# Cross-attention maxima in another order, with down tiles and late queries between them, in a fused two-layer decoder kernel

## The reference, cut to what matters

```python
x = x + block_attention(layernorm(x))            # 16 heads of 16, causal inside blocks of 64 tokens, rotary q and k
x = x + cross_attention(layernorm(x), ctx, ctx)  # below
x = x + ffn(layernorm(x))                        # routed experts, and a shared gated FFN
...
q = (Q @ Wq + bq).reshape(B, L, H, E)            # H = 16 heads, E = 16
k = (K @ Wk + bk).reshape(B, S, H, E)
scores = jnp.einsum('blhe,bshe->bhls', q, k)
A = jax.nn.softmax(scale * scores, axis=-1)
out = jnp.einsum('bhls,bshd->blhd', A, v).reshape(B, L, H * E) @ We + be
...
shared = jax.nn.gelu(sg, approximate=False) * su @ Sd.T
```

## Time and profile before

| | |
|---|---|
| median of 3 runs | 3006.3 us (3000.59 to 3008.07) |
| the profiled execution's own time | 3005.41 us |
| its span in the profile | 3003.6 us |
| mean granted clock of TensorE | 0.928 of full |
| busy: PE, PEld, DVE, ACT, POOL | 89%, 53%, 48%, 36%, 23% |
| span of the second layer's four batches | about 1740 to 2540 us |

### The profile page before, as it was taken

How to read it: one execution, slowest core, us unless ns; L and a number is a source line. 1 busy time by engine, 2 the same in 40 slices (tenths; PEclk the granted TensorE clock), 3 DMA queues, 4 the chain that set the end, 5 groups by cost and what they waited for, 6 DMA issues and landing times. The chain is left out here.

```text
span 3003.6 us, 40190 instructions
## 1 busy us (share of the span) xinstructions
PE 2674.7 (89%) x16417; PEld 1586.3 (53%) x16417; DVE 1450.4 (48%) x2233; ACT 1085.8 (36%) x1885; POOL 682.3 (23%) x364
## 2 busy tenths in 40 slices
PE   7679999999999999999959969989989898699997
PEld 4255534754275425653248844453552543487776
DVE  5565346832875366733711135445444553644432
ACT  4673245622563255523412223343434433011111
POOL 0255034900663055702520020000000000022222
PEclk8889999999999999999969977998989998799999
DMA  5540002100030003100059810010100102044442
GB/s 193 215 163 22 0 1 109 44 1 0 7 138 8 1 1 118 35 0 1 8 209 348 324 45 8 8 29 8 22 22 1 22 8 87 17 150 149 168 163 67
DMA packets 62127, 219.26 MB, mean 73 GB/s; under 512 B 12293, under 2 KB 28122, under 8 KB 45178
## 3 DMA queue, kind: packets, MB, share of 16 engines
q1 hardware_dynamic: 45802, 187.39, 17.3%
q0 software_dynamic: 9568, 18.75, 2.5%
q10 hardware_dynamic: 6576, 10.57, 1.0%
HBM read 172.50 MB, written 39.99 MB: 71 GB/s over the span
## 5 line engine op out<-in xcount | busy, mean ns | idle before, releaser
L642 PE MATMUL psum<-arena 128*128 128x256 f32 (+7 forms) x4224 | 1109.0, 414 | 65.4 <-ACT arena L1500 11.5
L642 PEld LDWEIGHTS psum<-arena 128*128 128x128 f32 (+1 forms) x4224 | 690.4, 199 | 433.9 <-issue 320.3
L2460 POOL TENSOR_TENSOR arena<-arena 128x1024 f32<-128x1024 f32 x128 | 300.1, 2386 | 111.7 <-DVE arena L1963 96.4
L1963 DVE TENSOR_TENSOR_SCAN arena<-arena,psum 128x512 f32<-128x512 f32 x256 | 291.5, 1201 | 26.3 <-PE psum L783 18.1
L783 PEld LDWEIGHTS psum<-arena 128*128 128x128 f32 x2048 | 243.0, 198 | 47.6 <-ACT arena L1530 40.3
L783 PE MATMUL psum<-arena 128*128 128x128 f32 x2048 | 253.7, 283 | 1.9 <-issue 1.9
L2495 POOL DMA_INDIRECT arena<-xn,arena x32 | 31.6, 989 | 921.8 <-DVE arena L2402 870.6
L2467 POOL TENSOR_TENSOR arena<-arena 128x1024 f32<-128x1024 f32 x32 | 76.0, 2376 | 654.6 <-ACT arena L1618 654.6
L2057 DVE SCALAR_TENSOR_TENSOR arena<-psum,arena 128x1024 f32<-128x1024 f32 x128 | 156.9, 1244 | 80.4 <-PE psum L928 80.1
L1618 ACT ACTIVATE arena<-arena 128x1024 f32<-128x1024 f32 x128 | 146.7, 1146 | 110.1 <-DVE arena L2057 109.9
L1224 PE MATMUL psum<-arena 32*128 32x512 f32 x512 | 179.4, 699 | 3.1 <-DVE arena L2253 3.1
(11 more groups left out here) (289 smaller groups left out, 2985.3 us busy)
## 6 DMA issues: line engine op xcount, KB each, us to landing
arena<-in_W SPq DMA_DIRECT2D x46, 1024.0 KB
arena<-c_rows SPq DMA_DIRECT2D x32, 512.0 KB, 3.7
arena<-in_Wg SPq DMA_DIRECT2D x16, 1024.0 KB
arena<-in_Wu SPq DMA_DIRECT2D x16, 1024.0 KB
arena<-in_Wd SPq DMA_DIRECT2D x16, 1024.0 KB
arena<-in_xT SPq DMA_DIRECT2D x8, 512.0 KB, 5.4
zs_all<-arena SPq DMA_DIRECT2D x4, 1024.0 KB, 3.9
ut_all<-arena SPq DMA_DIRECT2D x4, 1024.0 KB, 8.8
```

The costliest lines, as they stand in the source:

```text
L642: r = mm(dst, w, x, start=i == 0, stop=i == len(pairs) - 1)
L1963: V.tensor_tensor_scan(hs[n % 3][:, c, :], dA[n % 2][:, c, :], bank[4 + c], 0.0, ALU.mult, ALU.add)\
L2460: nc.gpsimd.tensor_tensor(h, h, c_all[:, n % CBUFS, :].unsqueeze(1).broadcast_to([P, 2, L]), ALU.mult)\
```

## The change

- The 64 maxima get a written order `MAXIMA`. 34 of them (groups 0 and 1, and two tiles of group 2) are made ahead of the loop; the other 30 go into steps 0 to 19 as 2, 1, 1, 2, picked so that their row groups are mostly those that the step's `scores_less_max` leaves free.
- Key tiles move from the norm into the block attention's end: two ahead of the last `weigh_blocks`, one ahead of and one behind the last `transpose_pair`.
- The down tiles 0 and 1 move into the norm in their place, 2 and 3 behind the first and the second four maxima, with bank 2 for the latter instead of 7.
- Query tiles 2 and 3 move behind maxima 21 and 27 (`late_queries`, lane `LQ`, bank 0); ACT evicts the last behind exponential 0, and maximum 32 waits for it.
- `block_scores` reads 32 rows of `rqT` and `rkT`, of which the upper 16 are zero; VectorE clears both once at the start of the second layer, and the first norm's buffers get words of their own.

The diff, with repeated edits of lane names left out:

```diff
-MAX_AHEAD = 24
+MAX_AHEAD = 34
+def _maxima():
+    tiles = [(g, n // 4, n % 4) for g in range(2) for n in range(16)] + [(2, 0, 0), (2, 0, 2)]
+    left = [(g, n // 4, n % 4) for g in (2, 3) for n in range(16) if (g, n // 4, n % 4) not in tiles]
+    steps = []
+    for v in range(32):
+        rows, now = ((0, 1), (2, 3))[v % 2], []
+        for _ in range(min((2, 1, 1, 2)[v % 4], len(left))):
+            group = [t for t in left if t[0] == left[0][0]]
+            apart = [t for t in group if t[2] in rows and t[2] not in [m[2] for m in now]]
+            now.append((apart + group)[0])
+            left.remove(now[-1])
+        steps.append(list(range(len(tiles), len(tiles) + len(now))))
+        tiles += now
+    return tiles, steps
...
-FFN_AT, OUT_AT = (2, 4, 6, 4), (6, 7)
+FFN_AT, OUT_AT = (2, 4, 6, 4), (6, 2)
...
-        xc0, sq0 = take(KD, L, at=blocks_at), take(KD, L, at=blocks_at + 2 * L)
+        xc0, sq0 = take(KD, L), take(KD, L)
...
-                   rounds(("v2_", 2), ("pair", 3 * NC), ("yk", 4), ("yq", 4), ("xn", 2)))
+                   rounds(("v2_", 2), ("pair", 3 * NC - 1), ("yk", 3), ("last", 2), ("yq", 2), ("xn", 2)))
...
+        LQ = Lane(sig("yq_tile"), sig("yq_drained"), bank[0:1], (("yq", 2),))
...
-                                       rqT[32 * j:32 * j + LE, g, o:o + BLK], rkT[32 * j:32 * j + LE, g, o:o + BLK],
+                                       rqT[32 * j:32 * j + 32, g, o:o + BLK], rkT[32 * j:32 * j + 32, g, o:o + BLK],
...
-                    elif f >= 0:
-                        ffn_out(f, 0)
-                        ffn_out(f, 1)
+                    elif p + 1 == NC:
+                        for g in range(2):
+                            project(LBA, f"yk{b}", g, w_yk, ctxB)
...
-                if f >= 0:
-                    ffn_out(f, 2)
+                project(LBA, f"yk{b}", 2, w_yk, ctxB)
                 transpose_pair(NC - 1)
-                if f >= 0:
-                    ffn_out(f, 3)
-                act_has(f"pair{b}", 3 * NC)
+                project(LBA, f"last{b}", 1, w_yk, ctxB, 3)
+                act_has(f"last{b}", 1)
...
                 norm_mean(x_b, 4)
-                for g in range(2):
-                    project(LBA, f"yk{b}", g, w_yk, ctxB)
+                if f >= 0:
+                    ffn_out(f, 0)
                 norm_var(mid_norm(b), sq, 5)
-                project(LBA, f"yk{b}", 2, w_yk, ctxB)
                 norm_rows(mid_norm(b), sd, 4)
-                project(LBA, f"yk{b}", 3, w_yk, ctxB)
+                if f >= 0:
+                    ffn_out(f, 1)
...
+                act_has(f"yq{b}", 1)
+                if f >= 0:
+                    w0(LFA.drained, LFA.upto(f"out{f}", 1))
                 for qc in range(NC):
-                    if qc == 0:
-                        act_has(f"yq{b}", 1)
-                    if qc >= 2:
-                        project(LBA, f"yq{b}", qc, w_yq, xn)
-                    for u in range(NC * qc, NC * (qc + 1)):
-                        scores_for_max(u)
-                act_has(f"yq{b}", 4)
+                    for n in range(NC * qc, NC * (qc + 1)):
+                        scores_for_max(n)
+                    if f >= 0 and qc < 2:
+                        ffn_out(f, 2 + qc)
+                act_has(f"yq{b}", 2)
+                if f >= 0:
+                    w0(LFA.drained, LFA.upto(f"out{f}", 2))
                 scores_for_max(16)
                 scores_for_max(17)
                 rows_of_max(0)
-                for u in range(18, MAX_AHEAD):
-                    scores_for_max(u)
+                for n in range(18, 22):
+                    scores_for_max(n)
+                late_queries(0)
+                scores_for_max(22)
+                scores_for_max(23)
                 scores_less_max(0)
+                for n in range(24, 28):
+                    scores_for_max(n)
+                late_queries(1)
+                for n in range(28, MAX_AHEAD):
+                    if n == 2 * LH:
+                        w(LQ.drained, 2)
+                    scores_for_max(n)
                 for v in range(V1):
                     g, i = v // 8, v % 8
                     if v + 1 < V1:
                         scores_less_max(v + 1)
-                    for u in range(MAX_AHEAD + 2 * v, min(MAX_AHEAD + 2 * v + 2, U1)):
-                        scores_for_max(u)
+                    for n in MAX_STEPS[v]:
+                        scores_for_max(n)
...
+                w(b_step, 3 * 2 + 3)
+                keys_in(0)
+                keys_in(1)
+                w(b_step, 3 * 3 + 3)
+                keys_in(2)
+                drain_pair(NC - 1)
+                keys_in(3)
+                norm_squares(mid_norm(b), xc, sq)
+                norm_root(mid_norm(b), sd, 5)
                 if f >= 0:
                     drain_out(f, 0)
+                for g in range(2):
+                    queries_in(g, LBA.take(act, 0, f"yq{b}", g), LBA.drained)
+                if f >= 0:
+                    drain_out(f, 1)
+                queries_in(2, LQ.take(act, b, "yq", 0), LQ.drained)
...
+                    if v == 0:
+                        queries_in(3, LQ.take(act, b, "yq", 1), LQ.drained)
...
+            V.memset(rqT, 0.0)
+            V.memset(rkT, 0.0)
             add_y(0)
```

More of the change, by code:

```diff
@@ L28 @@
 PT_AT, OT_AT = (0, 2, 5, 8), (4, 7, 10, 11)
-MAX_AHEAD = 24
+MAX_AHEAD = 34
 PICK_AT, PARTS_AT, AHEAD = 2, 4, CH // 2
 W1_AT = 3
+def _maxima():
[12 more added lines that the diff above has]
+    return tiles, steps
+MAXIMA, MAX_STEPS = _maxima()
 def _cross_tiles():
-    order = [("max", 16), ("max", 17), ("row", 0)] + [("max", u) for u in range(18, MAX_AHEAD)]
+    order = [("max", 16), ("max", 17), ("row", 0)] + [("max", n) for n in range(18, MAX_AHEAD)]
     for v in range(32):
-        order += [("max", u) for u in range(MAX_AHEAD + 2 * v, min(MAX_AHEAD + 2 * v + 2, 64))]
+        order += [("max", n) for n in MAX_STEPS[v]]
         if v % 8 == 3 and v > 8:
@@ L618, in _ @@
                 if b + 1 < B:
-                    sp.wait_ge(LBA.full.sem, LBA.full.at(LBA.upto(f"yk{b}", 4)))
+                    sp.wait_ge(LBA.full.sem, LBA.full.at(LBA.upto(f"last{b}", 2)))
                     load_ctx(b + 1)
@@ L1153, in transpose_pair @@
                     w(bo_step, 2 * (p + 1))
-                    t = LBA.fill(pe, 0, f"pair{b}", OT_AT[p])
+                    t = LBA.fill(pe, 0, *((f"pair{b}", OT_AT[p]) if p + 1 < NC else (f"last{b}", 0)))
                     for k in range(KD):
@@ L1213, in _, with scores_for_max, late_queries @@
                     project(LBA, f"yq{b}", g, w_yq, xn)
-                def scores_for_max(u):
-                    g, qc, j = u // LH, u // 4 % NC, u % 4
-                    if u < LH:
-                        if u >= 4:
-                            w(s1_max, u - 3)
+                def scores_for_max(n):
+                    g, qc, j = MAXIMA[n]
+                    if n < LH:
+                        if n >= 4:
+                            w(s1_max, n - 3)
                         t = bank[4 + j]
                     else:
-                        t = LBM.fill(pe, b, ("max", u))
+                        t = LBM.fill(pe, b, ("max", n))
                     mm(t, q4[32 * j:32 * j + 32, g, qc * P:(qc + 1) * P], k4[32 * j:32 * j + 32, g, :],
-                       start=True, stop=True).then_inc((s1_full if u < LH else LBM.full).sem, 1)
+                       start=True, stop=True).then_inc((s1_full if n < LH else LBM.full).sem, 1)
+                def late_queries(i):
+                    acc(LQ.fill(pe, b, "yq", i), [(w_yq[:, k, (2 + i) * P:(3 + i) * P], xn[:, k, :]) for k in range(KD)])\
+                        .then_inc(LQ.full.sem, 1)
                 def rows_of_max(g):
@@ L1231, in rows_of_max @@
                     else:
[L1232 removed]
+                        w(LBM.drained, LBM.upto(("max", last_max[g])))
                     t = LBM.fill(pe, b, ("row", g))
@@ L1700, in drain_pair @@
                 def drain_pair(p):
-                    t = LBA.take(act, 0, f"pair{b}", OT_AT[p])
+                    t = LBA.take(act, 0, *((f"pair{b}", OT_AT[p]) if p + 1 < NC else (f"last{b}", 0)))
                     A_(oT1[:, :, p * P:(p + 1) * P], t[:, 0:D].rearrange("p (k n) -> p k n", k=KD), ACT.Identity)\
@@ L1722, in _, with keys_in, queries_in @@
                         ffn_gelu(f, p + 1)
+                def keys_in(g):
+                    t = LBA.take(act, 0, *((f"yk{b}", g) if g < 3 else (f"last{b}", 1)))
+                    A_(k4[:, g, :], t, ACT.Identity, bias=vec[:, V_BK + g:V_BK + g + 1]).then_inc(LBA.drained.sem, 1)
+                def queries_in(g, t, done):
+                    A_(q4[:, g, :], t, ACT.Identity, bias=vec[:, V_BQ + g:V_BQ + g + 1]).then_inc(done.sem, 1)
+                w(b_step, 3 * 2 + 3)
[7 more added lines that the diff above has]
+                norm_root(mid_norm(b), sd, 5)
                 if f >= 0:
                     drain_out(f, 0)
```

(5 more changed lines are left out.)

26 lines of the change are left out of this document (6 added, 20 removed).

## The result

| | before | after |
|---|---|---|
| median of 15 runs each, taken together | 3000.19 us (2991.69 to 3008.07) | 3013.71 us (3005.41 to 3018.01) |
| ratio, with its 95% interval | | 1.0036 (1.0027 to 1.0046) |
| span of the profiled execution | 3003.6 us | 3008.9 us |

The change makes the kernel slower by 0.36%, some 11 us by the ratio: just beyond the 0.3% mark and inside the range of 2985 to 3030. The ratio is an estimate of its own; the medians of the table lie 13.5 us apart. The two profiled executions are only 5.3 us apart.

What follows compares the result with a forecast made beforehand. Bound: with four maxima a pair, a PSUM bank; with none, the chain scores, exponential, weighing; VectorE or banks ahead. Sum +2.9 - 6.9 + 5.4 = +1.4 us on 3005.4, 3006.8; median 3007.7, range 2985 to 3030.

Steps and rivals of the forecast that it cites:

- Pairs of steps: Head loop: with three maxima a pair, each finds its bank drained, so a pair takes 3.25 us instead of 4.02.
- The third rival: Head loop: pairs stay at 4.02 us because something else holds the weighing; 31 us more, 3039; chance 0.05.
- Phase ahead: First maximum to loop: ten more maxima and two late queries turn 24.6 us into 34.0 in batches 1 to 3.
- The late queries: Ahead of the loop: VectorE idles 2.2 us per query at the high clock, 4.7 at the low; 2.8 each taken, +5.6.
- a clock far from 0.8: Ahead of the loop: a granted clock far from 0.8 over this phase would show the prediction wrong.
- the rivals' cases: Ahead of the loop: clock stays high, 2988 us, chance 0.30; or low through both late queries, 3038 at worst, 0.22.
- for a loop entered at the low clock: Start of the head loop: a lump of 0.6 us a batch within the loop's 35.8 us.
- the second rival: Ahead of the loop: clock stays low through both late queries, loop enters low; 7.5 us a batch, 3038 at worst; chance 0.22.
- Keys behind block weights: Block scores to first maximum: moved keys gain 2.3 us in each of batches 1 to 3 (-6.9), cost batch 0 +5.4.
- the terms 2.0 + 7.0 + 0.8 + 3.8: Norm, batches 1 to 3: chain, rest of down tile 1, queries 0 and 1 make 13.8 us instead of 14.9, -1.1.
- the case that the prediction had named and left out of its sum: Norm, batches 1 to 3: if TensorE's 1.9 us of idle drop the clock, 1.7 us of the gain are lost.
- Block scores over 32 rows: Block attention: price between 0 (or a gain) and 11.7 us; 0 taken, as nearest to the 16-row shape.

Runs made afterwards that it cites:

- e1: The kernel before with only the new order and 34 maxima ahead; queries, keys and down tiles stay: 3015.08 us, 1.0029 of before.
- e10: The whole change with eight ahead maxima in banks 4 to 7 and late queries behind maxima 23 and 28: 2987.22 us, 0.9930 of before.
- e5: The changed kernel with block scores over 16 rows again, clearing writes kept: 3019.07 us, 1.0070 of before.
- e2: The kernel before with only the key and down tiles moved; 16 rows, old order of maxima: 3009.12 us, 1.0009 of before.
- e12: e10 with batch 0's keys back in its norm, as before: 2978.16 us, 0.9909 of before.
- e8: e3 with the keys moved behind block weights in batches 1 to 3 only: 2997.78 us, 0.9996 of before.
- e3: The kernel before with only block scores over 32 rows, the memsets and the norm buffers' own words: 2994.94 us, 0.9966 of before.
- e6: e3 with maxima 18 to 21 in banks 4 to 7, still 24 ahead in the old order: 2981.55 us, 0.9944 of before.

## Why the prediction was right and wrong

The measured time lies in the stated range, and above its centre; "slower" had 0.27, less than "same". Two misses of opposite sign, 10.8 us in the loop and 5.2 in the stage before it, cancel by half, and that is luck.

**Pairs of steps: right.** Forecast 3.25 us instead of 4.02; measured 3.25, with a row tile or flip 3.61 (forecast 3.55), last pair 5.08 (5.05). The third rival is out.

**Phase ahead: right in sum, its terms off against each other.** Forecast 34.0 us, 32.0 in batch 0; measured 33.4 in all four. The late queries cost 4.48 + 2.28 = 6.8 us of idle where 5.6 was put: the first ran at the low level (its bound was 4.7), the second at the high one (2.2). The maxima behind them came out cheaper than 0.70, at 0.63 and 0.64 in two rows of six, because they ran at the high level; waits of 0.97 and more are left in batch 0 alone. The two down tiles leave 0.96 and 1.20 us idle where 1.0 each was put. The prediction named a clock far from 0.8 as a sign of being wrong; it was 0.73 in batch 0 and 0.88 or 0.89 in the others. The clock was neither of the rivals' cases but one of each in every batch.

**Entering the loop: the step that failed.** The prediction allowed 0.6 us a batch "for a loop entered at the low clock". All four loops were entered low, and the first pair took 6.37 us instead of the 3.4 or so of the kernels that enter high. The loop is 38.5 for 35.8, 10.8 us in the four batches, and with it the stretch is +13.4 and not +2.9. The mechanism was named, in the sum and in the second rival, and its size was wrong by a factor of five; rows for it stood in the trace of before, where exponentials 1 to 3 take 5.1 us. Where they enter high, e1 and e10 have 35.55 and 35.07, so the other terms of the loop's sum hold. The closest comparison is inside e5, whose code from the first maximum on is that of after: batch 2 goes from exponential 1 to 3 in 3.61 us and has the loop of the forecast, batch 3 takes 6.20 (windows of both loops):

```profile
2273.00:2308.70 35.70, 32.72 (x238) 10.84 (x233) 21.97 (x36) 20.66 (x22) 0.00 (x0) 0.99 0.01 1
2469.60:2507.90 38.30, 35.32 (x239) 11.18 (x233) 22.07 (x36) 20.69 (x22) 0.00 (x0) 0.93 0.00 1
```

The same code has both loops, and the clock differs. The phase ahead of that batch 2 is 1.5 us longer than in after (34.9), so half of the 2.7 was paid there. The kernel went to the second rival's side, by its entry and by one of its two queries.
"TensorE: Matmul & The Clock Gate" of the Trainium skill, A second HAM failure mode, describes clock swings from small idles of TensorE while PSUM banks are cycled. The prediction took the 0.97 us of the earlier trace rows as agreeing, but those are idles of VectorE; TensorE is busy for all 2.90 us of e1's window at 0.50, so its small idles are not seen here. The swings are, and the banks bear on them: e10, which is after with more banks in turn and the late queries moved by a place or two, enters all four loops high, where after enters all four low.

**Keys behind block weights: signs right batch by batch, wrong in sum.** Without the 32 rows the stage takes 1.9 (e5) and 4.0 us (e2) more than before in the four batches, where the forecast was -1.5. Batch 0 forecast +5.4, measured +6.2 (e2: +7.5; e12 against e10: 4.6). The other batches forecast -2.3 each, measured -2.5, -4.4 and -6.0, but e2 without the 32 rows has only -1.2 on average. The chain of the norm gave 1.7 (first maximum 23.7 us behind the last weighing, 25.4 before) instead of 1.1; the terms 2.0 + 7.0 + 0.8 + 3.8 make 13.6 and not 13.8, so 1.3 by the prediction's own sum. In e2's batches 2 and 3 that gain is gone, by the case that the prediction had named and left out of its sum. In e8, whose loops behind moved down tiles are entered low in two of three batches, the move gains nothing; but in e2, with the same move, all four loops are entered high (42.8 us each), so that it lowers the entry is not shown.

**Block scores over 32 rows: wrong.** Priced at 0 with "a gain" left open and nothing to size it by. The 0 was right for the block scores themselves (0.91 us either way). The kernel gains 0.34% by them alone (e3) and as much inside the change (1.0070 to 1.0036), about 10 us, though not in e8 against e2. Without this part the change would have been slower by 0.7%. Memsets, norm buffers, SP's queue and ACT's new waits show nowhere: 0, as forecast.

**The sum.** By stages forecast +1.4, measured +6.7: loop +10.8, ahead -0.4, stage pre -5.2 (by e5 the 32 rows gave 8.6 there, and the keys cost 3.4 more than forecast). The miss of 5.3 is most of the 6.0 between 3007.7 and the median of 3013.71. The ratio says more, 11 us, because later runs of before lay lower than the first three: 3000.19 against the 3006.3 on which the forecast stood. What makes up the 4 us between ratio and stages is open; the runs of after alone spread over 13 us. Open too is why the level falls just where it does: no run here sets the clock, and e5 and e3 have it differ between batches of the same code.

## What to carry to other kernels

Before a row of small matmuls is moved ahead of a loop, look at what paces it: with three banks a maximum ahead cost 0.95 us at the low level and 0.63 at the high one, with seven 0.61 even at the low one, and freeing 0.77 in each pair does not pay for 0.95. Price the entry of a loop by its first iterations at the level at which the stretch ahead ends, not by a lump; here that was 3 us of every loop that was entered low. Time each part of a bundled change by itself: one part of this one lost 0.3%, one gave 0.3%, and the kernel with the lowest ratio (e12, 2978.16 us, 0.9909 of before) keeps the order, the 32 rows and the late queries, and adds the banks; e6, with the old order and four more banks, is at 0.9944 and not clearly behind.

## What was unexpected of the hardware

Sixty-four matmul instructions of block scores take 0.91 us with 16 rows and with 32, zeros in the added half, yet the granted clock of the stretch went from 0.92 to 0.97 and 1.00 in batches 2 and 3 (e5 against after), the same work then taking 3.5 and 5 us less, and the whole kernel 0.34% less, twice. Yet e12 has 0.92 with 32 rows as well. Whether zero rows act on the clock at all, and how, is not shown. And six maxima took 3.68 us, 0.61 each, at the low level in e6, where three banks at the same level give 0.95 (e1) and at the high level 0.63 (after): neither the low level alone nor the three banks alone slow the maxima, the two together do.
